# New order strings for all five engines, and a semaphore of its own for the last token statistic

## What is computed

```python
# tokens, per image (deformable sampling on a 32x32 grid, 8 points x 8 heads)
q_feat = bilinear_sample(x, grid)                       # (1024, 64)
h      = gelu(layer_norm(q_feat @ W_o1 + b_o1, ln_g, ln_b))
off    = (h @ W_o2 + b_o2) * 4                          # 8 points, x and y
sampled = bilinear_sample(x, grid + off * scale)        # (1024, 8, 64)
k, v   = sampled @ W_k.T, sampled @ W_v.T
tok    = softmax(q . k / sqrt(8), over the 8 points) @ v
h = concatenate([tok, txt])                             # 1152 tokens of 64
h = h + causal_attention(_layernorm(h))                 # one head of 64
# 16 experts (64 -> 128 -> 64, relu), the best 2 of each token
h = h + layernorm(y + sum_top2(gate * expert(y))) * gamma + beta, with y = _layernorm(h)
```

## Time and profile before

| | |
|---|---|
| time, median of 3 runs | 4566.16 us (4557.32 to 4566.56) |
| span of the profiled execution | 6851.9 us, 83914 instructions |
| busy in it: TensorE matmul, VectorE, GpSimd, ScalarE | 4265.1, 3165.0, 3077.1, 2222.4 us |
| mean granted TensorE clock | 0.734 of full |
| DMA | 911.33 MB; 30.0% and 15.5% of 16 engines' span in the two queues |

### The profile page before, as it was taken

How to read it: one execution, slowest core, us unless ns; L and a number is a source line. 1 busy time by engine, 2 the same in 40 slices (tenths; PEclk the granted TensorE clock), 3 DMA queues, 4 the chain that set the end, 5 groups by cost and what they waited for, 6 DMA issues and landing times.

```text
span 6851.9 us, 83914 instructions
## 1 busy us (share of the span) xinstructions
PE 4265.1 (62%) x26592; PEld 3681.7 (54%) x26592; DVE 3165.0 (46%) x10220; ACT 2222.4 (32%) x5378; POOL 3077.1 (45%) x3089
## 2 busy tenths in 40 slices
PE   3566765657566575665766667565765757656664
PEld 2555655646455464654656556454654646545543
DVE  1455445354454534545354544534545454544521
ACT  1333332323333332332333323333333333322321
POOL 2554454444534445354454544445344444545331
PEclk9777777777767776786777767777777777767765
DMA  6754443635536354353545536254353545433122
GB/s 194 216 154 136 145 135 115 177 96 157 148 103 189 86 174 119 118 165 94 175 118 160 144 106 190 84 176 119 118 164 93 175 113 152 138 106 89 54 59 67
DMA packets 938637, 911.33 MB, mean 133 GB/s; under 512 B 121306, under 2 KB 822362, under 8 KB 938072
## 3 DMA queue, kind: packets, MB, share of 16 engines
q1 hardware_dynamic: 805768, 598.22, 30.0%
q0 software_dynamic: 132432, 307.74, 15.5%
HBM read 583.69 MB, written 323.53 MB: 132 GB/s over the span
## 4 chain that ended last, share of the span: by engine, by line
another core or an unknown queue 31%; PE 29%; DVE 14%; issue 13%; ACT 10%; SPq 1%; DMA 1%; POOL 0%; DVEq 0%; POOLq 0%; ACTq 0%
PE ps L867 4%; PE ps L881 4%; PE ps L1024 3%; PE ps L1032 3%; PE ps L812 3%; PE ps L964 3%; PE ps L942 2%; ACT rows L1048 2%; ACT xm L1128 2%; DVE prod L1229 1%; PE ps L954 1%; PE ps L1006 1%; PE ps L823 1%; ACT kv_sb L1048 1%
## 5 line engine op out<-in xcount | busy, mean ns | idle before, releaser
L758 POOL DMA_INDIRECT gath<-table,idx x2048 | 2048.2, 1000 | 2909.6 <-issue 1211.3
L881 PE MATMUL ps<-w_kv,samp_t 128*128 128x128 f32 x4096 | 702.9, 323 | 166.6 <-issue 88.1
L867 PE MATMUL ps<-const,prod 128*128 128x128 f32 x4096 | 684.4, 322 | 168.8 <-issue 81.7
L964 PE MATMUL ps<-v_sb,probs_t 128*128 128x64 f32 x2880 | 455.2, 307 | 476.9 <-issue 223.1
L881 PEld LDWEIGHTS ps<-w_kv,samp_t 128*128 128x128 f32 x4096 | 637.0, 234 | 201.0 <-issue 130.5
L964 PEld LDWEIGHTS ps<-v_sb,probs_t 128*128 128x128 f32 x2880 | 442.9, 229 | 544.2 <-issue 303.5
L867 PEld LDWEIGHTS ps<-const,prod 128*128 128x128 f32 x4096 | 596.5, 172 | 202.7 <-issue 152.4
L774 POOL DMA_INDIRECT xs_d<-xm,row x512 | 525.9, 1027 | 392.7 <-DVE row L1229 231.6
L790 POOL DMA_INDIRECT ya<-ys_d,row x512 | 493.4, 964 | 454.4 <-DMA ys_d<-yx 268.6
L1229 DVE TENSOR_TENSOR prod<-gath,corner_w 128x1024 f32<-128x1024 f32 x512 | 619.9, 1219 | 159.3 <-remote 70.6
L942 PE MATMUL ps<-k_t,q_t 128*128 128x512 f32 (+3 forms) x960 | 479.7, 592 | 181.6 <-ACT v_sb L1048 76.5
(11 more groups left out here) (171 smaller groups left out, 6593.0 us busy)
## 6 DMA issues: line engine op xcount, KB each, us to landing
table<-rows SPq DMA_DIRECT2D x224, 1024.0 KB
fm<-in_x SPq DMA_DIRECT2D x256, 512.0 KB
wx<-w_d SPq DMA_DIRECT2D x768, 128.0 KB
gath<-table,idx POOLq DMA_INDIRECT x2048
wx<-w_d SPq DMA_DIRECT2D x64, 512.0 KB
table<-rows SPq DMA_DIRECT2D x32, 960.0 KB
xg<-xs_d SPq DMA_DIRECT2D x192, 130.0 KB
ys_d<-yx SPq DMA_DIRECT2D x192, 128.0 KB
```

The source lines that it names most:

```text
L758: pool.indirect_dma_start(out=gath[:, n % NG, p, :], out_offset=None, in_=tables[par], in_offset=bass.IndirectOffsetOnAxis(ap=idx[:, par, ...
L867: last = pe.matmul(bank(0, p * P, p * P + P), prod[h][:, (p * 2 + dx) * P:(p * 2 + dx + 1) * P], ident, is_transpose=True, start=(dx == 0) ...
L881: last = pe.matmul(bank(1, p * P, p * P + P), samp_t[n % 2][:, (4 * h + p) * P:(4 * h + p + 1) * P], w_kv[:], start=True, stop=True)
L964: last = pe.matmul(bank(7, (i % 8) * C, (i % 8) * C + C), probs_t[n % 3][:, (k % 4) * P:(k % 4) * P + P], v_sb[:, k, :], start=(k == 0), s ...
```

## The change

It replaces the strings of all five engines, in `TURNS` and in `LAST`. Each new string holds the same letters in the same numbers; only their order differs. Beside that, the last token tile's bn_stats (k = 0, t = 7) raises a signal of its own, `bn_ok`, instead of VectorE's common counter, and `moments` of the first layer norm waits for it.

```diff
--- before.py
+++ after.py
@@ -239,50 +239,51 @@
 
 FIRST_PART = TXG + 3
 TURNS = {
+    "sync":
+        "gghgggxxxxxxxxgxxggxxgxxggxxxxgggggggggehggggxxxxxxxxxxe",
+    "gpsimd":
+        "pppppppffffffffffffffffpffffffffffffffffpppccccccccccccccccccccccccccccccccppppp",
     "tensor":
-        "xxtxtkxtkxgtgakgatxgaaaxgagxssxtkgqxsatxgsqxsgkgxqtxgkgsxgagxagxtxsgsqgxkgtxgaxgkgxqsxgqsxtqkxtagsqa"
-        "xtxkgsagqtgkgaqtgssqagsqakqgaaqaqagagkggtgaagkagkgagtgkggtgkgtgkgtgrgkgtgxgkgtgxkgxagaxgaaatasxsksqs"
-        "axqtsaxqksxaqsgtxsqasgqxkaastqsxsqktkxaxaqxkxqsaqxssqatxaqkqtqxakaxaatxtxkxktaxkaaxaxx",
+        "xgxgxgtgktgktxgatxkxtkxtxtxtkxtxkxgtxgkxgkxgtxgkxgxgtxgakxgaxgkgaxgkaxgsxgtxgaxgsxssqksqgtqgktgakgts"
+        "gaqkgatssqgassqgassqgatqgaqssqgqgakqgasgakgaqgaqgaqatagkgtgkgtaaktagtagkgtgkggrgtgtxgxgxgxgaaxgtaxax"
+        "axaxssxssxqgqxsxqgxaxasaqssxsxsqaqqaqassqassqakqaskqtaqtxqaxkxkxqtxkxktxaxtxakakaakaaa",
     "scalar":
-        "xxttkxtagkgatxgaaaaagtaxgagvkxstqsxgkxgtsgvqgxqkgxggstgxgkxgtgsxqvgxkgsggxqtxkqtqkgxtvxsqggktggqtsqg"
-        "vkqggqskqgqqggtggaagvkaagkagatvgkggtgkggtgkgtvgaktgggkgtgxgkvagxagagatagakxaaeeeavstsqxgqskqtssqxgqv"
-        "kqkxtsqstkexqtkeeqxsvqqqxstkvqqktqvxxtkxtkxaavktaakaaxvxa",
+        "xgxggtgktaagktxaatxgkvtkxtxttkxvxtkgtxgkxvgkgtxgvkxggtxagkxgvagkgaxkgaxvggstxgaxgsqskqgtqgktgkgstvgq"
+        "kgstqgsqgsvqgtqgqsqggqkgqgskgqgeqeeqvgtgkgtgkaataaagtagktgkgtgagggtgtxgxgaagxgaaagaxaaxagsxsqgqsxvqx"
+        "sqsxsqqqqsqskqkqtsqvtqxkqxvktxktxkvtxqxtkvkeeeakaaavkaaav",
     "vector":
-        "wawaaxawwaaaaaaaaaaawvvxwwvvaaxvvwaavvvvvvxavavxaavwaawaavxvvvavawxwavvvaxaavvvwwvvavvvvaxvvvvaawaav"
-        "waaavvvavavvaawaaaaaaaaaaaaaaaavwvvvvvvveveeeaaavaeeeeaaawwavvavvveaeveeeevaaaraavvevvwaewrvraraeara"
-        "rvavvaaaaaaaraavevrrrrvvrxrwwvrgggggggggggvgeeegxggggggeeeeegggwegvaxvgaexvvexaaagvaggxxaevaaaxxavav"
-        "vvwxaxxaavaevvvxavxeeeeeeeggeeeaeeewxaeevevgeeeaeeeveexgxaagxxageexxexgxxgavxavwaaxvavvvxvvawvvvvvvv"
-        "avxxawvxvvavwaxaaaaaaaawaaaaaavvvvvvxvvvvvvvvaaaaaaaaxaaaavvaaa",
-    "gpsimd":
-        "pppppppffffffffffffffffpppffffffffffffffffccccccccccccccccccccccccccccccccpppppp",
-    "sync":
-        "ggxxgxxgxgxxxggxgxgxxhxgxxxgggggggggggxxgehgxgxxxexxxxxx",
+        "waawaaaaaaaaaaaaawxwwvwvvvvxwvwvvvwxwvvvvvvvxwwvvvvvvxvvvvvvwvvxvvwvvvvvxvvvvvvvvaxvwvvaxawvwavaavvw"
+        "avaaaawaaavavavaavvvvvavaaaweeeaeaaaeeeaeeeaeaeeeeeeeeeeeeeeeavavvvvveeawaaaaaaaaaaaaaaawewvvwveaaaa"
+        "aaeaaaaaaeraaaaaaaaaaaaawwrarrrrrrrrrraaaarrvvxvwwxxxgxxggggggggggggxgxxwxggggggggggxaaxxxgggvxaxxxv"
+        "eevxvxaxaaaxaaaaxaaagggggggagaaaaxaaaxxxvxxxavaaavavvveewavavvevvvvveevxvvewwvvvxvveevavavevvxvvveee"
+        "eeeeeeeeevvaaaaaaaaaaaaaaaavevvvvveevvvvvaaaaaavaaaaaavaaavvvvv",
 }
 LAST = {
+    "sync":
+        "hxxxxxxxxxxxxxxxxxhxexxxxxxexxxxxxxxxxxxxxxxxxxxxxexxxxxxxxxxxxxxxxxxxxxexxxxxee",
+    "gpsimd":
+        "ppppppffffffffffffffffpffffffffffffffffppccccccccccccccccccccccccccccccccpppffffffffffffffffffffffff"
+        "fffffffccccccccccccccccccccccccccccccccfffffffffffffffffffffffffffffffff",
     "tensor":
-        "xxtxtkxtkxtakatxaaaxaxssxtkqxsatxsqxskxqtxksxaxaxtxssqxktxaxkxqsxqsxtqkxtasqaxtxksaqtkaqtssqasqakqaa"
-        "qaqaaktaakakatktktktrktxktxkxaaxaaatasxsksqsaxqtsaxqksxaqstxsqasqxkaastqsxsqktkxaxaqxkxqsaqxssqatxaq"
-        "kqtqxakaxaatxtxkxktaxkaaxaxxxxxxxaaxaaaxaxssxqxsaxsqxsxqxsxaxaxxssqxxaxxqsxqsxqxasqaxxsaqaqssqasqaqa"
...
@@ -506,6 +507,7 @@
         kv_cp = sig("kv_cp", 4 * QT_N, 16)
         sc_sub = sig("sc_sub", 2 * QT_N)
         sc_exp = sig("sc_exp", 2 * QT_N, 16)
+        bn_ok = sig("bn_ok", 2)
         tok = sig("tok", 2 * QT_N, 24)
         txt_in = [sig(f"txt_in{n}", 16) for n in range(2)]
         ln_ab, end_ab = sig("ln_ab", 4), sig("end_ab", 2)
@@ -1438,10 +1440,16 @@
                 elif t == 0:
                     dve.wait_ge(*ya_rd.rise(pair, b + 1))
                 bn = (bn6, bn6_1, bn6_e)[k]
-                step(dve.bn_stats(bn[:, t, :], (h0[:, b], h1[:, par, b], out_sb)[k][:, t, :]))
+                last = dve.bn_stats(bn[:, t, :], (h0[:, b], h1[:, par, b], out_sb)[k][:, t, :])
+                if k == 0 and t == QT_N - 1:
+                    last.then_inc(bn_ok.sem, 1)
+                else:
+                    step(last)
 
             def moments(pair, par, b, k):
                 settle()
+                if k == 0:
+                    dve.wait_ge(*bn_ok.rise(pair, b + 1))
                 dve.sem_inc(dve_gate, 1)
                 for t in range(ST_N):
                     step(dve.bn_aggr((mv_e if k == 2 else mv)[:, t, :], (bn6, bn6_1, bn6_e)[k][:, t, :]))
```

More of the change, by code:

```diff
@@ L262 @@
     "tensor":
-        "xxtxtkxtkxtakatxaaaxaxssxtkqxsatxsqxskxqtxksxaxaxtxssqxktxaxkxqsxqsxtqkxtasqaxtxksaqtkaqtssqasqakqaa"
-        "qaqaaktaakakatktktktrktxktxkxaaxaaatasxsksqsaxqtsaxqksxaqstxsqasqxkaastqsxsqktkxaxaqxkxqsaqxssqatxaq"
-        "kqtqxakaxaatxtxkxktaxkaaxaxxxxxxxaaxaaaxaxssxqxsaxsqxsxqxsxaxaxxssqxxaxxqsxqsxqxasqaxxsaqaqssqasqaqa"
+        "xxxtktkatxatxtxtkxtxkxtxkxkxtkxtxkxtxkxtxkaxkaxkaxtsxaxkxssxsxqtxsqkqtaktaskqatssqassqaqassqaqssqatq"
+        "asqaktqaqaqktaaakttaaakkakraaaxaxaxtsxkxtaxtsxssxqkxsxqkxqtxkxaxasxqassqxssxqaqaqassassqaqaqxsaqxaqx"
@@ L271 @@
+        "aaakeeevkaakkaaaaaaaxaxvatxstakxtsvxqksxqkvqtxkxsqsqsxqvqqssqqqxsqxqqeeqxextkxtxktkxtxakavaxaaxatkxt"
+        "vxkxvxaxxaaaxaaxaaxaxasxsxqsxqxqsqsqsqqsqqsqqqsqqqaaaaaaaeeexxxxxxxxxxxxexeexxxxxxxxxxxxxxxxxxxxeeee"
         "ee",
     "vector":
[L273 to L275 removed]
@@ L283 @@
-    "sync":
-        "xxxxxxxxxxxxhxxxxxxehxxxxexxxxxxxxxxxxxxxxxxxxxxxxexxxxexxxxxxxxxxxxxxxxxxxxxxee",
+        "waawaaaaaaaaaaaaawxwwvvwwxvwvwvvxvvwvvvvvvxwvvvwvvvxvvvvvvvvwxwvvvvvvvvvvvvvxvawvvvvvxvaawxvvawaawav"
+        "aaaawaaaavavaaavaavvavvvvaaaawaevaaeevaeaeeeeeeeeewawaaaaaaaaaaaaaaaeeeeeeeeeeeeevvvvvveeevvaaaaaava"
+        "aaaaaeraaaaaaaaaaaaaaaaaavvrvrrrrrrrrrrwrwrvvevxvaxxwxwxxvevvvavxvxxxvavxxxvxvvvvvexvxxxvvevxaxaaaxa"
+        "aaaxaxaaxxxvvvxvaxaxaaaxaaavvveaaaeaeeevaaeaeeeeeeeeeeeexeeeawwaeeexwwaxaaaaaaaaaaaaaaavvvvxvwwvxvvv"
@@ L285 @@
+        "vvvvvvxvvvvaaaaaavaaaavaavvaaaaxvaaaaaaaaaaaaaaxxxaaaxaaaaaaaxaaaaaaaaaaaaaaaaaaaaaaaaaaaaaaaaaaaaae"
+        "eeeeeeeeeeeeeeaaaeaeaaaaaaaaraaaeeeeeeeeerrererrrrrrrrrrexxxxxxxxxxxxxxxxxxxxxxxxxxxxxxeeeeeeeeeeeee"
+        "eexeeeeeeeeeeexeeexxxxxxxxxxeeeeeeeeeeeeeeeeeeeeeeeeeeeeeeeeeeeeeeeeeeeeeeeeeeeeeeeeee",
 }
```

15 lines of the change are left out of this document (2 added, 13 removed).

## The result

The changed kernel takes 4603.99 us (median of 7 runs, 4581.9 to 4614.07), the kernel before in the same session 4566.56 (7 runs, 4557.32 to 4577.35): ratio 1.0075, 95% interval 1.0056 to 1.0093. It is slower by 0.75%; 4495 was forecast. The time lies inside the range, the direction is wrong.

What follows compares the result with a forecast made beforehand. GpSimd was the fullest queue, VectorE's waits were summed: -11.2 - 12 - 2.8 + 13.8 = -12.2 us per period, -183 over 15 periods, times 0.38 = 70; 4566 - 70 = 4496, rounded 4495. Range 4375 to 4660.

Steps and rivals of the forecast that it cites:

- signs named in advance: Changed kernel's trace: first score_max under 2 us, kq under 200, idx under 400, probs, pt_st and yx waits up to 25 more per period.
- The wait of 11.2 us goes: Start of the second sequence's attention: VectorE's wait before the first score_max vanishes, -11.2 us per period.
- Tokens: Round trip from weigh_rest to scores: late tiles better covered, half of 22.8 us saved, -12 us per period.
- The 2.8 us per period off the weighs' waits: Weighs run further ahead, so half of their 5.6 us of waits for gathers is saved, -2.8 us per period.
- The tight round trips: Less cover at score_max, exponential, experts and off_gelu: 27.6 us lost per period, half counted, +13.8.
- cover: VectorE's own work between the stage that starts a round trip over other engines and the stage needing its result.
- Some 24 us would be left: GpSimd's holes per period in the runs, beside 240 us of work in some 264 us.
- rival 3: GpSimd is the bound: the earlier idx gives back 12 x 15 = 180 us, 4386; chance 0.14.
- No loss: SyncE: first map chunk loads now stand behind the second sequence's store, not the expert load waiting for group 10; no cost.
- The last stretch: 783 us of the profile from the last idx on: counted as 0, with 20 us of the runs either way.
- rival 4: VectorE's weighs and GpSimd's gathers hold each other up: 34 of the 70 us lost, 4530; chance 0.03.
- rival 1: Slower: missing cover in score_max, exponential and experts paid in full, half the saved waits return, +83 us, 4650; chance 0.33.

Runs made afterwards that it cites:

- experiment 5: The changed kernel with expert stores 18 and 19 ahead of table 2 in SyncE's string; 4577.43 us, 1.0015 of the kernel before.
- 12: The kernel before with 30 small VectorE memsets per pair ahead of the routing marks; 4665.35 us, 1.0216.
- 13: The kernel before with 30 small VectorE memsets per pair ahead of expert_out of group 17; 4579.18 us, 1.0019.
- experiment 17: The changed kernel with expert stores 18 and 19 ahead of table 2 and neighbours exchanged in VectorE's string; 4566.34 us, 1.0002 of the kernel before.
- experiment 18: The kernel before with the new LAST and neighbours exchanged in its VectorE string; 4614.92 us, 1.0099.
- experiment 8: The kernel before with 7 of 8 gathers per tile, the eighth sample point counting as zero; 4482.77 us, 0.9803.
- Experiment 11: The kernel before with table 2 ahead of expert stores 18 and 19 in SyncE's string; 4573.52 us, 1.0017.
- experiment 2: The kernel before with only the new signal bn_ok, old strings kept; 4566.15 us, 0.9999.
- Experiments 9: The changed kernel with expert stores 18 and 19 ahead of table 2 and weigh_rest of tile 0 earlier in VectorE's string; 4573.58 us, 1.0019.
- experiments 1 to 4: The kernel before, unchanged (4570.94 us), or with the signal only (4566.15), the new TURNS only (4615.99), the new LAST only (4544.87).

## Why the prediction was wrong

**The profile that it was made from.** The caution at its end, that the waits of the profile may be of another kind than those of the runs, is what happened. The earlier trace rows spans 6851.9 us, the second profile of the same kernel 4568.9. The forecast took each wait at 0.38 of its size. They did not shrink evenly: GpSimd's wait for prod went from 940.3 to 57 us (0.06; 16.7 by the row that names it), kq for kv_sb from 364.1 to 78.0 (0.2), yx from 920.3 to 507.0 (0.55), all three in the groups or waits of the earlier trace rows. The first score_max of the second sequence waits 2.4 us on average in pairs 3 to 14, not 11.2. Part of the signs named in advance are met for the same reason and tell nothing: idx under 400 us and kq under 200 hold for the unchanged kernel's second profile too (129.0 and 78.0), and against that profile both rose (to 141.3 and 172.3). The first score_max did fall under 2 us, to 1.0 at most.

**The savings.** "The wait of 11.2 us goes" came true and could give 2.4 per period at best. "Tokens", 12 us per period, had 77.2/16 = 4.8 to save, and went the other way: kq for kv_sb is 172.3 us in the changed kernel. The late tiles 13 to 15, on whose cover the saving was built, had 4.3 us to save in all 16 pairs. In the changed kernel 126 of the 172.3 us stand at the sixth tile of a pair, which has 21 in the kernel before. The 2.8 us per period off the weighs' waits went the other way too: the idle time ahead of prod is 203.9 us in the second profile and 318.5 in the changed kernel.

**The losses.** The tight round trips, +13.8 per period, were put on score_max, the exponential and the experts. Of these only pt_st grew, by 15 us in the whole kernel; yx fell by 307 and probs by 84. The term has the wrong sign in these traces.

**The step that failed** is the one that turns VectorE's waits into time: "Nobody is short of work in these holes: an order decides who waits for whom. I therefore compare cover". VectorE's gaps over 0.35 us did shrink, by 115 us (1263.8 to 1148.8), more than the 70 us of the forecast, and the kernel got slower by 37. Experiments 5, 12, 13, 17 and 18 say the same: what an engine's idle time is worth depends on the place, and a filler there cost 0.1 to 1.1 of its length. In its place the runs show two chains of about equal length and a price on lateness: the waits ahead of experts 16 to 18 are all but gone in the changed kernel (0.2 us on average at 17 in the first 14 pairs, 8.9 before), but VectorE's last expert comes to the end of GpSimd's gathers instead of 7.5 us ahead of it, and GpSimd waits for its store, 71 us in all.

**GpSimd.** "Some 24 us would be left" per period pointed the right way, but was too large: between the first and the last idx of the second profile GpSimd is busy 2911.0 of 3825.8 us, and the 0.30 us behind each of 2781 instructions are 834 more, so 81 us are left over 15 periods, 5 each. A gather issue takes 1.045 us on average in that profile, not 0.96. From this row rival 3, "GpSimd is the bound", was true of the state, but its time, 4386, was built on a wait for idx that the runs do not have. The chain over VectorE would have stopped it well short anyway: 345 us less work on GpSimd gave 86 (experiment 8).

**SyncE.** "No loss" was worked out for the loads that move behind the stores. The place where table 2 moves ahead of the stores of experts 18 and 19 was not looked at, and it is the largest single item: 0.6% (experiment 5). Experiment 11 shows that the place alone is nearly free; it costs when the last expert comes near the end of the gathers, as it does with the new strings.

**The last stretch.** Taken as 0 within 20 us, because "the experts stand in the same order". It gave 0.4%: 29 us behind the last idx (622.3 to 593.1). The last routing's row is written at 4341.6 instead of 4367.4 us, and what follows takes 199 and 202 us. So the ranks of the last routing do end it, as said, and they came 26 us sooner; what came ahead of them was not only the 80 expert turns that I counted.

**Right** were the signal at 0 (experiment 2) and the small chance of rival 4: prod takes 1220 and 1221 ns in the two profiles. That the time lies inside the range is luck: the range reached so far up for the sake of rival 1, whose mechanism is not what happened, and none of the four terms of the sum measured what it was put at. "All busy times stay within 2%" failed by a little: VectorE +2.5%, ScalarE +4.0%. For VectorE that is the lost overlap of the table above, since the sum of its durations moved by 0.3%. Rival 1 has the sign of the result, not its mechanism: its round trips got shorter waits, not longer.

**Open.** What the new `TURNS` cost beside the stores, some 0.55%, is not settled. GpSimd's queue tells where it shows: from the first to the last idx experiment 5 takes 46 us longer than the second profile of the kernel before, made of 40 us of holes ahead of the first fetch and 29 more ahead of gathers, less 23 of shorter issues. So the last expert and the weighs come late to GpSimd; which exchange in the other strings makes them late was not found. Experiments 9 and 17 show that neither an earlier weigh nor fewer chains give it back.

A rival that no experiment took out is TensorE's clock, one of the signs named in the prediction. The changed kernel was granted 0.855 to 0.866 of full in its seven runs, the unchanged kernel 0.877 to 0.886 in the 17 runs beside experiments 1 to 4, and within the seven runs the time follows the clock (4581.9 us at 0.866, 4614.07 at 0.855). Whether the clock is a cause or goes with the same stalls these runs can't say. It is hardly the whole: experiment 17 ran at 0.874 on average against 0.861 for experiment 5, for 0.13%, and experiment 18 at 0.878 was 1% slower than the kernel before.

## What to carry to other kernels

Before summing waits, compare the span of the profile with the runs; where they differ by more than a per cent, take a second profile, for the waits did not survive the stretched execution, while most durations did (prod 1219 and 1220 ns; a gather's issue 1000 and 1045). A wait whose releaser the profile does not name is still a wait: compare where it ends with the instruction that it is known to need. In a kernel whose engines each follow a fixed order, a filler of 5 us at one place tells more than the idle time of an engine: it is paid in full, in part or not at all. A store that another engine waits for should be compared in the queue's order with everything that is moved ahead of it, even a table that nobody is late for.
